# Attention context moved between layouts by DMA instead of by transposes, in a four-layer kernel

## What is computed

```
p   = exp(scores - max)                     # 256 x 256 for each head
ctx = (p @ v) / sum(p)                      # divided by each query's sum
o   = ctx @ Wo                              # 512 x 512
x   = x + o * gate                          # gate: the feed-forward part's output
```

## Time and profile before

| | us |
|---|---|
| median of 3 runs | 1331.58 (1330.56 to 1336.55) |
| the profiled execution's own time | 1332.45 |
| its span (first to last instruction) | 1330.7 |
| round 0, slots (about) | 177 to 630 |
| round 1, slots (about) | 894 to 1267 |

### The profile page before, as it was taken

One profiled execution on the slowest core, in us unless ns is written; L12 is line 12 of the kernel. 1 busy time (PEld: TensorE's weight loads), 2 busy tenths in 40 slices (PEclk: granted clock), 3 DMA queues, 4 the chain that ended last, 5 costly groups with the idle time before them and its releaser, 6 DMA issues.

```text
span 1330.7 us, 22702 instructions
## 1 busy us (share of the span) xinstructions
PE 1216.5 (91%) x8860; PEld 900.0 (68%) x8860; DVE 808.3 (61%) x1322; ACT 652.6 (49%) x1106; POOL 385.9 (29%) x460
## 2 busy tenths in 40 slices
PE   4999999999999999979999999999899889898897
PEld 3788876666656556546777787776666666676664
DVE  8743467665675645674655566536776776765444
ACT  3333357555454555554333333336665655565653
POOL 1000125333210101021344434405532342424443
PEclk9999989999999999979999999899999999999999
DMA  6000000110000100001242222120001001000001
GB/s 254 0 1 0 1 34 3 48 58 2 1 2 2 36 1 1 26 25 48 72 142 95 95 72 80 64 80 3 2 2 40 2 2 34 1 25 23 2 1 63
DMA packets 15259, 48.07 MB, mean 36 GB/s; under 512 B 2858, under 2 KB 6959, under 8 KB 14388
## 3 DMA queue, kind: packets, MB, share of 16 engines
q1 hardware_dynamic: 15156, 46.63, 10.1%
HBM read 44.00 MB, written 2.10 MB: 35 GB/s over the span
## 4 chain that ended last, share of the span: by engine, by line
PE 71%; DVE 14%; ACT 8%; issue 4%; DMA 2%; POOL 0%; POOLq 0%; DVEq 0%; ACTq 0%; SPq 0%
PE bank L650 18%; PE bank L766 14%; PE bank L680 8%; PE bank L909 8%; PE bank L869 6%; PE bank L817 4%; PE bank L783 3%; DVE negmax L1816 3%; ACT probs L1381 3%; PE bank L849 2%; ACT pv L1389 2%; PE bank L880 2%; DMA W_lo_whole<-in_w 2%; PE bank L797 1%; PE bank L826 1%
## 5 line engine op out<-in xcount | busy, mean ns | idle before, releaser
L1816 DVE TENSOR_REDUCE negmax<-bank 128x4 f32<-128x1024 f32 (+1 forms) x256 | 250.3, 1017 | 77.0 <-PE bank L826 66.2
L1381 ACT ACTIVATE probs<-bank 128x1024 f32<-128x1024 f32 (+1 forms) x256 | 218.0, 865 | 46.0 <-PE bank L849 37.7
L2023 POOL TENSOR_SCALAR_AFFINE_SELECT probs<-probs 128x512 f32<-128x512 f32 x192 | 125.9, 666 | 292.3 <-ACT probs L1381 292.1
L1966 POOL TENSOR_TENSOR W_lo<-W_lo_whole,W_hi 128x1536 fp32r<-128x1536 f32 x28 | 98.4, 3516 | 155.8 <-ACT W_hi L1132 155.8
L817 PE MATMUL bank<-kT,qT 64*128 64x256 f32 (+1 forms) x1024 | 110.5, 312 | 30.1 <-DVE negmaxT L1834 8.8
L817 PEld LDWEIGHTS bank<-kT,qT 64*128 64x128 f32 x1024 | 81.4, 191 | 65.9 <-issue 33.2
L869 PE MATMUL bank<-probs,V 128*32 128x256 f32 (+1 forms) x2048 | 119.6, 352 | 6.6 <-DVE negmax L1816 5.1
L1389 ACT ACTIVATE pv<-bank 128x256 f32<-128x256 f32 x128 | 49.2, 384 | 154.1 <-PE bank L869 153.6
L849 PE MATMUL bank<-qT,kT 64*128 64x256 f32 (+1 forms) x640 | 113.4, 384 | 3.7 <-DVE h_lo_whole L1638 1.6
L1132 ACT ACTIVATE W_hi<-W_lo_whole 128x1536 fp32r<-128x1536 f32 x28 | 41.7, 1488 | 130.6 <-DVE W_lo_whole L1592 130.6
L650 PE MATMUL bank<-xT_hi,W_hi 128*128 128x512 f32 x224 | 91.7, 410 | 5.6 <-ACT silu L1145 4.5
(11 more groups left out here) (205 smaller groups left out, 2692.3 us busy)
## 6 DMA issues: line engine op xcount, KB each, us to landing
W_lo_whole<-in_w SPq DMA_DIRECT2D x28, 768.0 KB, 4.1
Wqkv_lo_whole<-in_Wqkv SPq DMA_DIRECT2D x6, 768.0 KB, 6.7
Wo_lo_whole<-in_Wo SPq DMA_DIRECT2D x4, 1024.0 KB, 4.9
Wqkv<-in_Wqkv SPq DMA_DIRECT2D x2, 1536.0 KB, 7.5
Wdown_whole<-in_Wd SPq DMA_DIRECT2D x1, 2816.0 KB, 14.6
x<-in_x SPq DMA_DIRECT2D x4, 512.0 KB, 5.4
out<-x SPq DMA_DIRECT2D x8, 256.0 KB, 2.0
V_lo_whole<-in_V SPq DMA_DIRECT2D x1, 1408.0 KB, 5.8
```

The lines of the kernel that those rows point to most:

```text
L1381: nc.scalar.activation(A[l].probs[gi % 2][kb][:, :, q0 - kb * A[l].probs1:].rearrange("p (b h) q -> p b h q", b=2), B.tensor(key)[:, :, 0: ...
L1816: v.tensor_reduce(A[l].negmax[u % 2][:, qb, :].rearrange("p (b h) -> p b h", b=2)[:, :, 2 * g:2 * g + 2], B.tensor(key)[:, :, 0:2 * nk].re ...
L1966: gp.tensor_tensor(lo, whole, hi.bitcast(F32), ALU.subtract).then_inc(w_low.sem, 1)
L2023: gp.affine_select(out=blk, in_=blk, compare_op=ALU.is_ge, fill=0.0, base=0, pattern=[[0, 4], [1, P]], channel_multiplier=-1).then_inc(cau ...
```

## The change

`turn_context`, `turn_rows`, `take_rows` and the low part on DVE go. SP moves each group's 64 context rows from `pv` to a compact layout with four DMAs, and with a fifth spreads each head's row of sums over its 16 partitions. Two groups make 128 partitions. DVE takes the reciprocal of 128x256 sums and multiplies 128x256, once for each pair, in the even slots from G = 4 on (pair q in slot 2q + 4), into a ring of six. In layers 0, 2 and 3 ACT copies the high part (`context_high`, behind `take_pv` in the same slot) and POOL forms the low part, last in its slot. `project_out` reads the ring. `take_pv` now waits for the moves of two groups before. The product of attention and gate goes to `gate`. SP's program is written out by slots, with the same loads. The bank of `weigh_values` is unchanged (`values_bank`).

```diff
-def context_bank(r, U):
-    return 6 if U < RUN - 1 else (5, 4)[r]
-def rows_turned(r, U, g):
...
+def pair_scaled(G):
+    return (G - 4) // 2 if G >= 4 and G % 2 == 0 else None
+WO3_SLOTS = {(10, 1): (0,), (10, 2): (1, 2), (10, 3): (3,)}
...
+        def moved(r, G):
+            return pv_moved[G % 2], 16 * MOVES * ((RUN * GROUPS * r + G) // 2 + 1)
...
 PE, project_out
-                pe.wait_ge(*B.emptied(("ctxT", l, b, tau)))
+                pe.wait_ge(*(ctx_low if GQA[l] else ctx_scaled).at(l, 4 * (b + 1)))
 PE, slot
-                if G >= 2:
-                    turn_context(r, G - 2, G)
-                for n in rows_turned(r, U, g):
-                    turn_rows(*n, OUT_BANK[n[2]])
 PE, ffn2
-                turn_context(0, last - 1, last)
-                turn_context(0, last, last, 2)
                 down(2, 0)
-                turn_rows(1, SEQS - 1, 0, 3)
-                turn_rows(1, SEQS - 1, 1, 2)
 ACT, take_pv
+                if G >= 2:
+                    act.wait_ge(*moved(r, G - 2))
                 nc.scalar.activation(A[l].pv[gi % 2][:], B.tensor(key)[:, 0:SEQ], copy).then_inc(B.empties(key), 1)
-            def take_rows(l, b, tau):
...
+            def context_high(r, q):
+                l, qi = pair(r, q)
+                if GQA[l]:
+                    act.wait_ge(*ctx_scaled.at(l, qi + 1))
+                    nc.scalar.activation(ctx_hi[r][:, q % RING, :], ctx_whole[r][:, q % RING, :], copy).then_inc(ctx_high.sem, 1)
 ACT, slot
                 if G >= 1:
                     take_pv(r, G - 1)
+                if pair_scaled(G) is not None:
+                    context_high(r, pair_scaled(G))
 DVE
-            def context(r, G):
...
+            def context(r, q):
+                l, qi = pair(r, q)
+                dve.wait_ge(*moved(r, 2 * q))
+                dve.wait_ge(*moved(r, 2 * q + 1))
+                sums = A[l].sums[q % 2][:]
+                v.reciprocal(sums, sums).then_inc(rs_ready.sem, 1)
+                if q >= RING:
+                    ll, qq = pair(r, q - RING)
+                    dve.wait_ge(*B.filled(("O", ll, qq // 4, 1)))
+                dve.wait_ge(*rs_ready.at(l, qi + 1))
+                v.tensor_tensor(ctx_whole[r][:, q % RING, :], A[l].parts[q % 2][:], sums, ALU.mult).then_inc(ctx_scaled.sem, 1)
 DVE, slot (same place in the slot)
-                if G >= 2:
-                    context(r, G - 2)
+                if pair_scaled(G) is not None:
+                    context(r, pair_scaled(G))
...
-                for n in rows_turned(r, U, g):
-                    if GQA[n[0]]:
-                        context_low(*n)
 POOL
+            def context_low(r, q):
+                l, qi = pair(r, q)
+                if GQA[l]:
+                    pool.wait_ge(*ctx_high.at(l, qi + 1))
+                    gp.tensor_tensor(ctx_lo[r][:, q % RING, :], ctx_whole[r][:, q % RING, :],
+                                     ctx_hi[r][:, q % RING, :].bitcast(F32), ALU.subtract).then_inc(ctx_low.sem, 1)
 SP
+            def move_values(r, G):
+                l, gi = group(r, G)
+                q = G // 2
+                sp.wait_ge(*B.emptied(("PV", l, gi)))
+                if q >= 2:
+                    ll, qq = pair(r, q - 2)
+                    sp.wait_ge(*ctx_scaled.at(ll, qq + 1))
+                pv, row, first = A[l].pv[gi % 2], SEQ, 64 * (G % 2)
+                for i in range(4):
+                    load(A[l].parts[q % 2][first + HD * i:first + HD * (i + 1), :], pv[32 * i:32 * i + HD, :], pv_moved[G % 2])
+                load(A[l].sums[q % 2][first:first + 64, :], bass.AP(pv, HD * row, [[32 * row, 4], [0, HD], [1, SEQ]]), pv_moved[G % 2])
...
+            def slot(r, G):
+                U, g = divmod(G, GROUPS)
+                if g == 2 and U + 1 < RUN:
+                    place_maxima(r, U + 1)
+                if r == 0 and g == 3:
+                    loads_0(U + 1)
...
+                if G >= 1:
+                    move_values(r, G - 1)
+                if r == 1 and g == 3:
+                    loads_1(U + 1)
```

More of the change, by code:

```diff
@@ L51 @@
 CELL = HD + 4
+RING = 6
+MOVES = 5
 NEG = -1.0e30
@@ L433, in program @@
         assert at[0] <= R + 102496
-        at = [R + first["ctxT_lo"]]
+        at = [names["ctxT0_hi"][0]]
         tanh1 = [place(f"tanh1_{i}", [P, D], F32, at) for i in range(2)]
@@ L503, in program @@
         m_rows = [sem(f"max_rows_placed{i}") for i in range(2)]
+        pv_moved = [sem(f"weighed_values_moved{i}") for i in range(2)]
         out_done = sem("output_stored")
@@ L872, in weigh_values @@
                 ins.then_inc(B.fills(key), 1)
[L874 to L888, removed]
-                ins.then_inc(B.fills(key), 1)
             def project_out(l, b, tau, bank):
@@ L1068, in ffn3 @@
                     if e == CHUNKS3_EARLY:
-                        turn_context(1, last - 1, last)
                         weigh_values(1, last, last)
-                    if e == CHUNKS3_EARLY + 1:
-                        turn_context(1, last, last)
-                        for tau in range(2):
-                            turn_rows(3, SEQS - 1, tau, 6 + tau)
-                    if e == CHUNKS3_EARLY + 2:
+                    if e == CHUNKS3_EARLY + 3:
                         for tau in range(2):
@@ L1259, in ffn2 @@
                 gate_silu(2, CHUNKS2_EARLY)
-                for tau in range(2):
-                    take_rows(1, SEQS - 1, tau)
                 weights_high(CHUNKS2_EARLY + 1)
@@ L1306, in ffn3 @@
                     if e == CHUNKS3_EARLY + 1:
-                        for tau in range(2):
-                            take_rows(3, SEQS - 1, tau)
+                        context_high(1, RUN * GROUPS // 2 - 2)
+                    if e == CHUNKS3_EARLY + 2:
+                        context_high(1, RUN * GROUPS // 2 - 1)
                         bias2_high()
@@ L1760, in ffn3 @@
             def ffn3():
-                last = RUN * GROUPS - 1
+                last = RUN * GROUPS // 2 - 1
                 for e in range(CHUNKS3_EARLY, 2 * HC3):
@@ L1768, in ffn3 @@
                         context(1, last)
-                        for tau in range(2):
-                            context_low(3, SEQS - 1, tau)
-                    if e == CHUNKS3_EARLY + 2:
+                    if e == CHUNKS3_EARLY + 3:
                         for tau in range(2):
@@ L2037, in slot @@
                     wqkv_low_part(3, g)
-                if r == 1 and U == 10:
-                    wo_low_part(3, g)
+                if r == 1:
+                    for c in WO3_SLOTS.get((U, g), ()):
+                        wo_low_part(3, c)
                 if r == 1 and (U, g) in SPLIT3_SLOTS:
@@ L2051, in slot @@
                     wo_low_part(2 * r, g)
+                if pair_scaled(G) is not None:
+                    context_low(r, pair_scaled(G))
             def ffn2():
```

157 lines of the change are left out of this document (73 added, 84 removed).

## The result

The changed kernel takes 1362.61 us (median of 4 runs, 1359.97 to 1368.37) against 1332.74 us (4 runs, 1330.56 to 1336.55): a ratio of 1.0227, interval 1.0185 to 1.0268. It is 30 us slower. 1332 was forecast, and the range ended at 1357.

The account below looks back on a forecast made before the run. PE was taken to bound the kernel (busy 91% of the span, 71% of the chain), DVE setting some short slots. Terms 27.8 - 10.8 - 5.0 - 2.7 - 5.7 - 2.5 = +1.1 us gave 1332 us, no change; range 1305 to 1357.

Parts of the forecast that it names:

- 27.8 - 10.8 - 5.0 - 2.7: Layers 0, 2, 3: even slots +27.8 us, odd slots -10.8, ten fourth-group slots -5.0, DVE sooner in late first-group slots -2.7.
- first- and third-group slots: Even slots of the grouped-query layers, where the scaling delays ACT's next exponential; less DVE coming sooner: +25.1 us.
- the others: Grouped-query layers: 47 odd slots save 0.23 us each, ten fourth-group slots lose four L888 transposes: -15.8 us.
- The late first-group slot: Even units' first slots, where DVE reaches the scaling late behind rope and statistics: seven cost 2.0 to 2.5 us each.
- The chosen mechanism: Slots with `context_high`: ACT waits for DVE's scaling, delaying the next exponential and PE's bank 2; 46 slots, +27.8 us together.
- Layer 1 needs no split, so ACT waits for nothing ... -5.7: Layer 1: dropped transposes save 8.7 us; two third-group slots with the reciprocal ahead of `take_max` cost 1.5 each.
- the tails, -2.5: Ends behind the rounds: about -3 us from PE's wait and transposes, partly given back by DMA and scaling ahead of `project_out`.
- Rival 1: DVE's reciprocal is dear, 8.3 ns an element, and 27 waiting slots pass it on: 1343 us; decides at 2.13 us; chance 0.21.
- Rival 2: SP's five DMAs behind `place_maxima` land late, some 15 units wait 1.5 us: +23, 1356 us; chance 0.11.
- Rival 3: DVE's reciprocal is cheap: 1323 us at 1.55 us, 1299 at the multiply's price, 1320 as one case; chance 0.31.
- Rival 4: Freed PE time gains nothing, since banks set the odd slots too; only waits remain, about +15, 1347 us; chance 0.06.

Follow-up runs that it names:

- e13: Changed kernel plus idle TensorE transposes of the identity inside fifteen of its waits, no work removed: 1350.55 us (ratio 1.0129).
- e1: Changed kernel with ACT's `context_high` moved behind the next slot's two exponentials and POOL's low half behind that slot's cuts: 1357.58 us (1.0168).
- e5: e1 with DVE's scaling of the pair moved from the middle of its slot to the end: 1335.51 us (1.0014).
- e3: Changed kernel with the four moves of 16 context rows made one of 64 rows (wrong rows), the sums' move kept: 1356.94 us (1.0164).
- e8: Changed kernel with the reciprocal taken of only 128 of the 256 columns: 1326.59 us (0.9943).
- e2: Changed kernel with the reciprocal of the sums and the wait for it left out: 1299.49 us (0.9731).
- e11: e5 with some scalings moved to units' second slots, behind row maxima, and the sums' DMA issued first on its own semaphore: 1320.05 us (0.9909).

## Why the prediction was wrong

*The sizes at its base were right.* Reciprocal 1744 ns for 1.92 us, multiply 0.425 for 0.43 except in seven of 64, `context_high` 0.41 for 0.42, ACT's wait 30.1 us in 27 slots. The Trainium skill (VectorE: DVE Perf Modes, section Walkthrough: the 8-slice pipeline in each mode) with its repeat count of 8 had given an estimate of 2.13 us; the trace doesn't agree, and the measurement decides, 1744 ns or 6.25 ns an element over the base.

*The grouped-query layers came out right by luck.* The forecast for them was 27.8 - 10.8 - 5.0 - 2.7 = +9.3 us; the windows show -1.4 + 9.4 = +8.0. Its parts missed both ways: first- and third-group slots measured +16.5 where +25.1 was forecast, the others -8.6 where -15.8 was. The late first-group slot cost +1.0 (1.6.0: 4.30 to 5.34 us), not +2.5. And round 1's +9.4 holds a clock of 0.95 for 0.99; e13 takes 6.3 us of it away. The chosen mechanism, `max(end of take_pv, start of scaling + 2.35)` ahead of the exponential, was real, but taking it away (e1) gained about 8 us of 30, within the noise, since PE then waited for row maxima.

*Step that failed first: "Layer 1 needs no split, so ACT waits for nothing ... -5.7".* Measured +10.0. ACT indeed waits for nothing, but DVE's longer scaling stands ahead of `gate_tile1`, of the maxima and of the normalised tile. Slot 0.12.1 alone lost 3.0 us and 0.8.1 2.9, their units 3.7 and 4.7. In unit 14 the slots lost and gained by turns, +1.3 in all, in spite of the multiply of 3.5 us. In unit 15 slot 0.15.1 is 1.9 us longer with PE busy all through: there ACT's next exponentials come later, behind a weight copy that waits for DVE. I asked for every pair who waits for its *result*, and only in two slots what is queued *behind* it. e5 moved nothing but this, against e1, and got the stage from 261.6 back to 251.0 us; 0.15.1 stayed as it was. By e13, 3.2 of the +10.0 are clock.

*Second: the tails, -2.5.* Measured +3.1 and +6.5. I gave the scaling and five DMAs ahead of `project_out` "in part" for them. e3 shows the issues, with the clock that hangs on them, to be worth 7.5 us there, and e13 shows 6.1 us of the end to be clock.

*Third, a term that was not there: the granted clock.* The profile of before had it in view: the clock of 0.97 and 0.96 in the first two stages is there, and most of its stretches at 1.2 GHz lie at a wait of PE of about 1.3 us or more, as one of 3.13 us in slot 0.13.3. All but one of the changed kernel's twenty stretches do (the expectation of e1 says each does). A change that opens new waits can pay the clock again behind them. At 12 to 14 us it is nearly half of the loss; without it the time, 1350.55 us in e13, would have been inside the range, though some 18 us above the forecast. The Trainium skill (TensorE: Matmul & The Clock Gate, section What's actually happening) says that the slow clock is the default and that activity releases it; e13 agrees: transposes of an identity were activity enough in slot 0.12.1. Its section HAM oscillation counts half of the slow time as lost; slot 0.12.1 agrees while PE is busy (1.69 us), the runs of e5 show half of that, 6.7 us of 27, as PE is not what every slot waits for.

*The rivals.* Rival 1 had the right sign, 1343 us, from a dearer reciprocal; the reciprocal was cheaper than forecast and its *price* higher. It decides, by e8 and the changed kernel, at about 1.08 us, not at 2.13. Rival 2 did not come: DVE waited 7.8 us in all for the moves, 6.4 of it in the two feed-forward parts behind the rounds, and the first packets of the earlier trace rows flow 1.0 us behind the issue, not 1.3. Rival 3, a cheap reciprocal, was a sound mechanism with its point of decision misplaced and its gain overstated: the 1299 us that it has for a reciprocal at the multiply's price came only with none at all (e2, 1299.5); on the line between e2 and e8, 0.43 us would give about 1312, an estimate. Rival 4 had its own sign, odd slots that are not shorter, and it did not come: 38 of the 47 odd slots of the grouped-query layers are shorter, 8.6 us in all. How much of e2's gain of 36 us is freed PE time stays open, since DVE, too, has less to do there than in the kernel before (771 us busy for 808).

## What to carry to other kernels

Cost an added operation by what is queued behind it on its engine, slot by slot, not by who waits for its result: with the same instructions, moving the scaling behind the short operations that PE waits for was worth 22 us and a second step 10, while removing the visible 30 us wait for its result was worth about 8, within the noise. An engine that is busy 65% of the span can be full in every second slot; the price of a microsecond on it, clock included, went from 0.45 to 0.89 as it filled. Read the spread of a new operation's times, not its mean alone: two of 64 held most of the excess. When a change opens waits of over a microsecond on TensorE, give the granted clock a term of its own, and try to fill the waits that can't be removed.

## What the runs showed of the hardware

A reciprocal on DVE took 944 ns for 128 and 1744 ns for 256 elements a partition, against 425 ns for the multiply of 256, both inputs in SBUF. Beside a POOL operation of 3.4 us with both inputs in SBUF two of these multiplies took 3.5 us; the reciprocals kept their 1736 to 1753 ns beside POOL operations as well. The broadcast DMA of the sums was no dearer to issue than a plain one (0.60 us of SP for 0.59). TensorE waits of 1.3 to 2.3 us were followed by a stretch at 1.2 GHz in some slots and not in others: in the changed kernel PE waits 1.39 us for the exponentials in 1.10.1 and in 1.6.1, and only the first has a stretch behind it. Filling a wait now and then moved the stretch to another slot. In slot 0.12.1 idle transposes of an identity held 2.4 GHz. Left open: whether e11's sums-first order is worth more than the 2 us that the profiles show, and how the 50 us between e2 and the changed kernel that are not clock divide over the slots; no run separates them.
